# The row maxima of causal attention in another order, with the waits for their transfers split in two

## What is computed

```python
t = _to_tokens(x)                                   # (8, 1024, 192)
q = (n @ Wq).reshape(b, s, 6, 32).transpose(0, 2, 1, 3)   # n = layernorm(t); k and v alike
scores = jnp.einsum('bhqd,bhkd->bhqk', q, k) / jnp.sqrt(32)
scores = jnp.where(causal, scores, -jnp.inf)
attn = jax.nn.softmax(scores, axis=-1)
out = jnp.einsum('bhqk,bhkd->bhqd', attn, v)
t = t + out.transpose(0, 2, 1, 3).reshape(b, s, 192) @ Wo + bo
```

## Time and profile before

| | us |
|---|---|
| three runs of the kernel, median | 1661.14 (1660.44 to 1661.31) |
| the profiled run | 1659.74 |
| its span, first to last instruction | 1657.7 |
| granted clock of TensorE, mean of the span | 0.996 |

### The profile page before, as it was taken

One profiled execution on the slowest core, in us unless ns is written; L12 is line 12 of the kernel. 1 busy time (PEld: TensorE's weight loads), 2 busy tenths in 40 slices (PEclk: granted clock), 3 DMA queues, 4 the chain that ended last, 5 costly groups with the idle time before them and its releaser, 6 DMA issues.

```text
span 1657.7 us, 32908 instructions
## 1 busy us (share of the span) xinstructions
PE 1586.3 (96%) x13274; PEld 1034.4 (62%) x13274; DVE 1188.0 (72%) x2537; ACT 904.0 (55%) x1329; POOL 173.5 (10%) x247
## 2 busy tenths in 40 slices
PE   3989999999999999999999999999999999999999
PEld 1534676657665576656766567665776557765676
DVE  6687786767776776867768678676777777686644
ACT  3217654466545665466554665446654566545665
POOL 2200102001210003000020010200121000300000
PEclk9999999999999999999999999999999999999999
DMA  4202002100111002010020100200011100200000
GB/s 162 59 25 65 1 1 68 35 16 2 41 28 49 1 1 68 1 49 1 1 68 1 50 2 1 67 26 25 1 38 32 49 1 1 68 1 11 1 11 10
DMA packets 25131, 47.30 MB, mean 29 GB/s; under 512 B 7410, under 2 KB 16946, under 8 KB 23700
## 3 DMA queue, kind: packets, MB, share of 16 engines
q1 hardware_dynamic: 15728, 27.85, 6.1%
q0 software_dynamic: 6144, 9.45, 2.4%
q10 hardware_dynamic: 3108, 7.91, 1.3%
HBM read 19.82 MB, written 6.29 MB: 16 GB/s over the span
## 4 chain that ended last, share of the span: by engine, by line
PE 73%; DVE 17%; ACT 5%; issue 2%; POOL 1%; DMA 1%; SPq 0%; DVEq 0%; ACTq 0%; POOLq 0%
PE ps L440 22%; PE ps L732 18%; PE ps L677 10%; PE ps L475 6%; DVE mx L1174 4%; PE ps L618 4%; PE ps L524 3%; DVE room L1361 3%; PE ps L447 2%; ACT room L900 2%; DVE norm_stats L1015 2%; ACT room L908 2%; DVE acc L1345 1%; PE ps L511 1%; PE ps L479 1%
## 5 line engine op out<-in xcount | busy, mean ns | idle before, releaser
L900 ACT ACTIVATE room<-ps,b_sb 128x512 f32<-128x512 f32 x384 | 263.1, 685 | 438.5 <-PE ps L440 438.4
L732 PE MATMUL ps<-wout_h,room 128*128 128x192 f16 x3072 | 457.2, 246 | 0.0
L1361 DVE SCALAR_TENSOR_TENSOR room<-room 128x512 f16<-128x512 f32 x384 | 263.2, 689 | 183.0 <-ACT room L908 180.8
L732 PE MATMUL ps<-wout_l,room 128*128 128x192 f16 x1536 | 377.4, 246 | 0.0
L732 PEld LDWEIGHTS ps<-wout_h,room 128*128 128x128 f16 x3072 | 285.9, 98 | 34.0 <-issue 3.2
L880 ACT ACTIVATE room<-ps 128x1024 f32<-128x1024 f32 (+3 forms) x288 | 224.8, 811 | 141.4 <-PE ps L479 104.0
L1174 DVE TENSOR_REDUCE mx<-ps 128x2 f32<-128x1024 f32 (+3 forms) x288 | 265.8, 953 | 33.7 <-PE ps L622 21.1
L908 ACT ACTIVATE room<-room 128x512 f16<-128x512 f32 x384 | 241.9, 630 | 33.6 <-PE ps L732 0.4
L677 PE MATMUL ps<-room,v 128*64 128x512 f32 (+3 forms) x1152 | 231.7, 486 | 0.9 <-DVE o L1306 0.9
L618 PE MATMUL ps<-qk 96*128 96x512 f16 (+3 forms) x576 | 151.0, 329 | 17.4 <-DVE mx L1174 10.6
L732 PEld LDWEIGHTS ps<-wout_l,room 128*128 128x128 f16 x1536 | 150.1, 98 | 27.1
(11 more groups left out here) (203 smaller groups left out, 2317.4 us busy)
## 6 DMA issues: line engine op xcount, KB each, us to landing
xc<-x_ch SPq DMA_DIRECT2D x8, 768.0 KB, 5.8
qk<-qk_all SPq DMA_DIRECT2D x96, 64.0 KB, 2.3
qk<-qk_all POOLq DMA_DIRECT2D x96, 64.0 KB, 2.5
out<-acc ACTq DMA_DIRECT2D x16, 384.0 KB, 2.6
xt<-x_tok SPq DMA_DIRECT2D x7, 768.0 KB, 7.1
qk<-qk_all POOLq DMA_DIRECT2D x96, 32.0 KB, 2.0
qk<-qk_all SPq DMA_DIRECT2D x96, 32.0 KB, 2.3
room<-w_in SPq DMA_DIRECT2D x2, 1024.0 KB, 8.5
```

Of the source, the lines that this page charges most:

```text
L732: mm = pe.matmul(dst, hid[:, s, tok], w[:, n, :], start=(k == 0 and m == 0 and t % 2 == 0), stop=False, skip_group_check=True)
L900: act.activation(h32[:, i % N_H, :], ps[:, H_BANK[i], :], ACT.Gelu, scale=1 / (U_SCALE * W_SCALE), bias=b1_sb[:, n:n + 1])\
L1361: V.scalar_tensor_tensor(out=h_l[:, s, :], in0=h32[:, s, :], scalar=A_SCALE, in1=h_h[:, s, :], op0=ALU.mult, op1=ALU.subtract)\
```

## The change

`M_ITEMS` is put in another order: within a block the pair of heads is outermost, in the order 0, 2, 1, then the tiles, then the halves. In block 0 the widths of the items are then 128, 256, 384, 512, three times over; in block 1 they are 512, 128, 512, 256, 512, 384, 512, 512 (the off-diagonal half first), three times over. `maximum_step(i)` and the number of idle products for a width stay as they are.

The semaphores `heads_in[b]` and `keys_in[b]` become two each: part 0 counts the six transfers of `r` 0 and 1, part 1 those of `r` 2 and 3. TensorE waits ahead of pair 0's first item for part 0 of both, ahead of pair 2's first item for part 1 of the keys (its queries came with part 0), and ahead of pair 1's first item for part 1 of the queries. The transfers themselves, their order and their size are the same.

```diff
-M_ITEMS = [(b, t, half, pair) for b in range(NB) for t in range(b * TB, (b + 1) * TB)
-           for half in range(b + 1) for pair in range(PAIRS)]
+M_ITEMS = [(b, t, half, pair) for b in range(NB) for pair in (0, 2, 1)
+           for t in range(b * TB, (b + 1) * TB) for half in range(b + 1)]
...
-        heads_in = [sem("heads_in0", 16 * 3 * 4), sem("heads_in1", 16 * 3 * 4)]
-        keys_in = [sem("keys_in0", 16 * 3 * 4), sem("keys_in1", 16 * 3 * 4)]
+        heads_in = [[sem(f"heads_in{b}{part}", 16 * 3 * 2) for part in range(2)] for b in range(NB)]
+        keys_in = [[sem(f"keys_in{b}{part}", 16 * 3 * 2) for part in range(2)] for b in range(NB)]
...
                             if r < 2:
                                 sp.dma_start(q4[dst, r:HEADS:4, tok], qk[row, q, 0:3:2, tok])\
-                                  .then_inc(heads_in[b], 16)
+                                  .then_inc(heads_in[b][0], 16)
                             else:
-                                sp.dma_start(q4[dst, r, tok], qk[row, q, 0, tok]).then_inc(heads_in[b], 16)
+                                sp.dma_start(q4[dst, r, tok], qk[row, q, 0, tok]).then_inc(heads_in[b][1], 16)
...
-                    if i == 0:
-                        pe.wait_ge(heads_in[0], at(heads_in[0], img, whole(heads_in[0])))
-                        pe.wait_ge(keys_in[0], at(keys_in[0], img, whole(keys_in[0])))
-                    if i == NM // 3:
-                        pe.wait_ge(heads_in[1], at(heads_in[1], img, whole(heads_in[1])))
-                        pe.wait_ge(keys_in[1], at(keys_in[1], img, whole(keys_in[1])))
+                    if t % TB == 0 and half == 0:
+
+                        if pair == 0:
+                            pe.wait_ge(heads_in[b][0], at(heads_in[b][0], img, whole(heads_in[b][0])))
+                            pe.wait_ge(keys_in[b][0], at(keys_in[b][0], img, whole(keys_in[b][0])))
+                        elif pair == 2:
+                            pe.wait_ge(keys_in[b][1], at(keys_in[b][1], img, whole(keys_in[b][1])))
+                        else:
+                            pe.wait_ge(heads_in[b][1], at(heads_in[b][1], img, whole(heads_in[b][1])))
```

More of the change, by code:

```diff
@@ L972, in spread_keys @@
                             if r < 2:
-                                pool.dma_start(k4[dst, r, tok], qk[row, k, 1, tok]).then_inc(keys_in[b], 16)
+                                pool.dma_start(k4[dst, r, tok], qk[row, k, 1, tok]).then_inc(keys_in[b][0], 16)
                             else:
                                 pool.dma_start(k4[dst, r:HEADS:2, tok], qk[row, k, 1:3, tok])\
-                                    .then_inc(keys_in[b], 16)
+                                    .then_inc(keys_in[b][1], 16)
             def attend(img):
```

## The result

| | before | after |
|---|---|---|
| median of seven runs, us | 1659.69 (1659.04 to 1661.31) | 1666.08 (1664.37 to 1667.12) |
| ratio of the times | | 1.0035 (95%: 1.0024 to 1.0047) |
| the profiled run | 1659.74 | 1664.37 |
| its span | 1657.7 | 1662.4 |

The change makes the kernel slower by 6.4 us in the median, 0.35%; the interval leaves out zero.

The account below looks back on a forecast made before the run. TensorE was taken as the bound over the maxima of later images, VectorE's reductions setting the pace in image 0. Later images +4.3 us and image 0 +0.6, +4.9 on a median of 1661.14, gave 1666.0 us; range 1662.2 to 1668.8.

Parts of the forecast that it names:

- Images 1 to 7: Maxima of each later image: TensorE waits 4.2 instead of 3.6 us, +0.61 us an image, +4.3 us in all.
- The chain: Steps 31 to 32: longer reduction of item 2 delays the expert's add, then item 3's reduction; item 5 waits 1.08, was 0.46.
- Passed on to the end: Behind the maxima: what follows is chained to TensorE, so the whole added wait reaches the end of the image.
- taken back later: Rival, chance 0.22: later waits absorb the 0.6 us an image, or item 5 finds the add no later; 1661.7 us.
- the backlog goes: Rival, chance 0.07: alternating widths let VectorE catch up before the rows of maxima and item 32; 1652.6 us.
- A reduction's pace: VectorE in the walk of all 36 items: a ready reduction starts 0.08 us before the previous one's recorded end.
- The waits for transfers: Four waits an image become eight at no cost; image 0's first maximum gains 0.2 us, not 3, behind 16 idle products.
- Image 0: Its maxima: last reduction ends at 119.55 instead of 119.03, +0.6 us with the clock kept; +1.3 if the clock falls.
- A first score ahead of 119.0: Sign of being wrong, in image 0; the forecast had the first score near 119.6 at full clock.
- Block 0's gaps: VectorE's gaps in image 0, block 0, idle products included: about 2.0 us against 0.9 for the old order.
- block 1's gaps: VectorE's gaps in image 0, block 1, before full-width reductions: 1.8 us against 0.55 for the old order.
- The clock's rule: Image 0: by the skill's advice neither order loses its clock, +0.6 us; by the row it can fall without gap, +1.3.

Follow-up runs that it names:

- the two edits that take item 5's wait away: Changed kernel with item 5 due half a step later, 1659.42 us (0.9992 of the old kernel); changed kernel with items 3 and 4 swapped, 1661.03 us (1.0006).
- the order alone: Changed kernel's new order of items with the old kernel's two whole waits for transfers: 1665.65 us, 1.0032 of the old kernel.
- the kernels that differ in block 0 alone: Image 0's pass: new order in both blocks 37.56 us against in block 1 only 36.43; new order in block 0 only 37.60 against old kernel 36.61.
- the pairs of kernels that differ in block 1 alone: Image 0's pass: new order in both blocks 37.56 us against in block 0 only 37.60; new order in block 1 only 36.43 against old kernel 36.61.
- all five kernels with the old block 1: Old kernel, and it with split waits, new order in block 0, no idle products ahead, or new due steps: 1659.69, 1660.05, 1664.04, 1662.92, 1638.35 us.
- the kernel with item 5 later: Changed kernel with item 5 due half a step later, behind expert_out and hidden: 1659.42 us, 0.9992 of the old kernel.
- All seven kernels with a pairwise block 1: Changed kernel; with whole waits; block 1 alone new; no idle products ahead; own due steps; item 5 later; items 3 and 4 swapped: 1641.77 to 1666.08 us.

## Why the prediction was right, and where it wasn't

*Direction and size.* Forecast 1666.0, measured 1666.08; the profiled run 1664.6 against 1664.37. The change itself was forecast at +4.9 us and is +6.4 in the medians, so the direction is right and the size is 1.5 short. That the absolute times meet within 0.1 us is luck: 1.4 us of the forecast carried over the distance of the profiled run from a median of three, and in seven runs that distance vanished (1659.69 and 1659.74). In the changed kernel a distance of 1.7 came from somewhere else, which the prediction had not thought of (below).

*Images 1 to 7.* +0.61 an image was forecast, +0.66 measured. The chain was right link by link: add at 266.18 (266.23), reduction of item 3 at 268.09 (268.12), item 5 at 269.37 (269.40). Item 2 waited 0.11 less and item 5 0.63 more (forecast 0.11 and 0.62), and the two edits that take item 5's wait away take the loss away. Of the later places the rows of maxima and item 18 come at 288.30 and 289.46 and item 32 at 309.18, with 0.61, 0.77 and 0.92 us of idle time ahead, where the earlier trace rows have 0.64, 0.80 and 0.82. The forecast had the sum of the first two smaller by 0.09 (1.65, was 1.74), and the waiting falls by 0.07 from step 36 to step 40. It had items 29 and 32 together longer by 0.19, and the waiting grows by 0.25 from step 44 to step 47.

*Passed on to the end.* Right. The lag stands at 0.66 from the end of the maxima into the next front, and the period has it. With that the rival "taken back later" falls, and so does "the backlog goes": it wanted fewer waits than 10.6 us, there were 18.0.

*A reduction's pace.* The walk let reductions succeed each other 0.08 us faster than they are recorded. The earlier trace rows bear that out on a longer run: the 12 from 106.05 are nine at 2x512 and three at 2x384, by the pace 9 x 1.14 + 3 x 0.875 + 0.08 = 12.97 us, by the recorded durations 9 x 1.22 + 3 x 0.953 = 13.84; the row has 12.87. The Trainium skill (Perfetto Trace Analysis, section "Optimizing Scalar/DVE Operations") says that part of a profiled latency, the acknowledgement of the write, overlaps with the next instruction. This trace agrees that successive reductions overlap in the records, by 0.08 us; what the overlapping part is it doesn't show.

*The waits for transfers.* Right. With the order alone the first maximum waits 0.23 us for the last transfer, in the changed kernel not at all; that is what the split is worth as it stands. The 3 us that the prediction put behind the idle products are there too, as the kernel without them shows. The added waits cost nothing that can be seen.

*Image 0.* The pass was to grow by 0.7 us (walk: 119.03 - 82.36 = 36.67 to 119.55 - 82.14 = 37.41) and grew by 0.94, to 37.55; the clock was to stay and stayed. The first score came at 119.01 and not 119.6, since the first maximum was early, at 81.46 and not 82.1; the front ahead of it, which the change doesn't touch, had run faster. A first score ahead of 119.0 was named as a sign of being wrong, and it was missed by 0.01 us only; with such a front that sign says nothing of the pass. The term that was mis-sized is block 1. Block 0's gaps were to cost 1.1 us more (2.0 against 0.9); the kernels that differ in block 0 alone say 37.56 - 36.43 = 1.13 and 37.60 - 36.61 = 0.99. Block 1's were to cost 1.25 more, less half a microsecond at item 18 and 1.06 for the clock: -0.3. By the pairs of kernels that differ in block 1 alone it is 37.56 - 37.60 = -0.04 and 36.43 - 36.61 = -0.18. So the sum was near, but the two halves that cancel in it were both too large: the clock cost 0.4 to 0.65 us (36.10 with idle products against 36.53, 36.61 and 36.75) and not 1.06, and block 1's gaps cost 0.33 and not 0.75 (36.43 - 36.10, if the added idle products cost nothing, which was not measured alone).

*The clock's rule.* The Trainium skill (TensorE: Matmul & The Clock Gate, section "Why this matters for your kernels") warns of long idle gaps between bursts. One fall here stands behind such a gap, the one behind the 3.58 us wait of the old kernel without idle products, and there the trace agrees. The fall between 97.4 and 99.5 us in all five kernels with the old block 1 is another matter: the longest idle time ahead of it is 0.72 to 0.75 us. The prediction took from that advice that without a long gap neither order would lose its clock; the advice doesn't promise that, and the rows that the prediction set beside it already showed the fall without a gap.

## What to carry to other kernels

When one engine fills double-buffered banks and a second empties them, an item's place is good or bad by what else the second engine has to do in that step: look for the item that waits, and ask which long reduction or foreign work stands ahead of its banks. Give each item a due step by its size and by the other work on the draining engine, before trying orders: here that was worth 22 us, and the order of the items less than 7. A wait that is split to let the first part through brings nothing while filler stands ahead of it, so take the two together or leave both.

## What the runs showed of the hardware

*The clock falls without a pause.* In image 0's pass the old kernel's TensorE had no idle time above 0.74 us ahead of the fall, and still the granted clock fell to 0.50 after a stretch in which it was busy for 1.96 of 3.40 us; in the changed kernel, with 2.92 of 3.40 and one wait of 0.94 us, it stayed at 1.00. All seven kernels with a pairwise block 1 kept it through the pass, all five with a tile-wise one lost it, and filler of two products at each short item kept it with the old order. Each of these is one profiled execution. What the chip looks at can't be told from this.

*The front of image 0 takes another course from kernel to kernel.* Its instructions up to the first maximum are the same in all these kernels but the two without the 16 idle products, yet the first maximum starts anywhere from 81.46 to 83.64. The granted clock differs ahead of it: half clock for 10.2 us (36.6 to 46.8) in the old kernel's profiled run and for 6.8 us (37.4 to 44.2) in the changed one's, and in some a further stretch, as in the kernel with item 5 later (window 62 to 70 us):

```profile
62.00:70.00 8.00, 5.91 (x27) 3.48 (x26) 5.73 (x15) 2.05 (x2) 0.41 (x1) 0.79 0.00 0
```

where the old and the changed kernel have 1.00. The five kernels with idle products that have this further stretch start their first maximum between 82.77 and 83.64, the six without it between 81.46 and 82.36. Two kernels, the one with the new order in block 0 alone and the one with items 3 and 4 swapped, also have half clock for 3.4 us just behind the first scores, from 121.3 and 121.1 us. The course differs between executions of one kernel as well: of the changed kernel's seven runs the two with a mean clock of 0.998 have spans of 1662.4, the other five, at 0.996 and 0.997, of 1663.5 to 1665.0. The profiled run is one of the two. That is the 1.7 us between its time and the median, and why 4.7 us of span became 6.4 of the median; that the clock in the front makes this difference is argued from the mean clock, as only one execution has a trace. What decides the course was not tried.
